# The last stage of a vision tower on one core: where the expert shares are spread, in what order a turn is issued, and when its weights are loaded

## The reference, cut to what matters

```
out = attention among the 8 heads' vectors, softmax(q.k * 16**-0.5) over the heads of one token, times v
y   = x + merge(heads) @ w_proj.T + b_proj           # heads regrouped over tokens
f   = layernorm(y) * ln_scale + ln_bias
routed: a group gate picks one of 2 groups, a softmax over its 4 experts, the top 2 of them, shares renormalised
shared = swiglu(f @ shared_in_w.T) @ shared_out_w.T + shared_out_b
h      = swiglu(f @ expert_in_w.T)                   # 256 values, the same for all 8 experts
y + shared + sum over e of share[e] * (h @ expert_out_weight[e].T + expert_out_bias[e])
```

## Time and profile before

| | |
|---|---|
| median of 3 runs | 2949.59 us |
| the profiled execution | 2955.88 us |
| its span | 2954.1 us |
| stage A, stage B, stage C (from the trace) | 0 to about 1580, to about 1921, to 2954 us |
| PE, DVE, POOL, ACT busy over the span | 83%, 83%, 67%, 51% |
| mean granted TensorE clock | 0.924 of full |

### The profile page before, as it was taken

The page is one execution under the profiler, slowest core; times in us unless marked ns, Lnnn a source line. Parts: engine busy times, 40 slices in busy tenths (PEclk is TensorE's granted clock), DMA queues, the critical chain, the costliest instruction groups (busy, mean ns, idle before and its releaser), DMA issues. The chain is left out here.

```text
span 2954.1 us, 25221 instructions
## 1 busy us (share of the span) xinstructions
PE 2455.6 (83%) x6718; PEld 1146.3 (39%) x6718; DVE 2447.7 (83%) x3527; ACT 1511.1 (51%) x2542; POOL 1978.0 (67%) x1008
## 2 busy tenths in 40 slices
PE   6899898898998898988973068438999999998998
PEld 2344444444444444444431033213444444444443
DVE  4999999999999999999997822137888888888875
ACT  5666666666666666676652134234444433443332
POOL 3888888888888887888882068755555555555540
PEclk9999999999999999999996579758999999999999
DMA  2333323323333323324231024310000000000000
GB/s 83 110 94 98 109 92 105 106 87 117 94 99 107 100 91 108 103 87 119 89 102 51 0 50 71 36 51 22 29 29 29 29 29 29 29 29 29 26 22 11
DMA packets 169758, 199.27 MB, mean 67 GB/s; under 512 B 38969, under 2 KB 156946, under 8 KB 169490
## 3 DMA queue, kind: packets, MB, share of 16 engines
q1 hardware_dynamic: 158354, 189.27, 20.9%
q0 software_dynamic: 11264, 8.40, 2.2%
HBM read 164.37 MB, written 33.25 MB: 67 GB/s over the span
## 5 line engine op out<-in xcount | busy, mean ns | idle before, releaser
L905 POOL TENSOR_TENSOR a_hc<-a_h,a_cs 128x896 f32<-128x896 f32 (+1 forms) x448 | 891.6, 2002 | 182.1 <-DVE a_h L744 181.2
L360 PE MATMUL a_y_bank<-a_hc,a_ident 128*128 128x448 f32 (+1 forms) x1792 | 766.7, 562 | 14.7 <-POOL a_hc L905 13.6
L537 ACT ACTIVATE a_da<-a_dt,a_neg_a 128x448 f32<-128x448 f32 (+1 forms) x896 | 548.4, 632 | 331.3 <-DVE a_h L744 330.3
L744 DVE TENSOR_TENSOR_SCAN a_h<-a_da,a_h,a_dbx 128x448 f32<-128x448 f32 x528 | 583.1, 1134 | 14.2 <-ACT a_da L537 11.9
L360 PEld LDWEIGHTS a_y_bank<-a_hc,a_ident 128*128 128x128 f32 x1792 | 344.1, 196 | 359.9 <-issue 287.2
L2086 POOL TENSOR_TENSOR c_prod<-c_prob,c_qkv 128x1024 f32<-128x1024 f32 x100 | 280.7, 2849 | 274.6 <-DVE c_prob L1973 274.6
L1670 PE MATMUL c_p_ACC<-c_sc,c_w_ex 128*128 128x512 f32 x800 | 365.4, 594 | 0.0
L2079 POOL TENSOR_TENSOR c_prod<-c_qkv 128x1024 f32<-128x1024 f32 x100 | 231.9, 2341 | 152.7 <-ACT c_qkv L1754 152.7
L728 DVE TENSOR_TENSOR a_dbx<-a_dtx,a_b_bank 128x896 f32<-128x896 f32 (+1 forms) x308 | 328.5, 1067 | 4.5 <-PE a_b_bank L353 0.7
L1947 DVE TENSOR_TENSOR c_sc<-c_hid,c_p_CB 128x1024 f32<-128x1024 f32 x200 | 239.9, 1214 | 69.6 <-PE c_p_CB L1662 67.1
L893 POOL TENSOR_TENSOR a_dbp<-a_dtx,a_bs 128x896 f32<-128x896 f32 (+1 forms) x140 | 269.7, 1936 | 0.3
(11 more groups left out here) (297 smaller groups left out, 3688.3 us busy)
## 6 DMA issues: line engine op xcount, KB each, us to landing
a_cs<-c_rows SPq DMA_DIRECT2D x96, 896.0 KB, 5.3
a_bs<-c_rows SPq DMA_DIRECT2D x24, 1120.0 KB, 5.7
a_cs<-c_rows SPq DMA_DIRECT2D x16, 900.0 KB, 4.4
c_x<-h_rows SPq DMA_DIRECT2D x25, 256.0 KB, 2.8
heads<-c_ot SPq DMA_DIRECT2D x25, 256.0 KB, 2.3
c_dealt<-heads SPq DMA_DIRECT2D x200, 32.0 KB, 1.9
rolled<-c_res SPq DMA_DIRECT2D x25, 256.0 KB, 2.1
h_rows<-a_th SPq DMA_DIRECT2D x24, 224.0 KB
```

Of the source, the lines that this page charges most:

```text
L360: pe.matmul(y_bank[:, d, 0:g.w], ident[:], hc[:, (g.i * NS + n) % HC_RING, d, 0:g.w], start=(n == 0), stop=(n == NS - 1)).then_inc(s_sum, 1)
L537: act.activation(da[:, k % DA_RING, 0:g.w], dt[g.slot][:, d, 0:g.w], ACT.Exp, scale=neg_a[:, d * NS + n:d * NS + n + 1]).then_inc(s_da, 1)
L744: dve.tensor_tensor_scan(h[:, n, d, 0:g.w], da[:, (g.i * 2 * NS + k) % DA_RING, 0:g.w], x, state, ALU.mult, ALU.add).then_inc(s_scan, 1)
L905: pool.tensor_tensor(hc[:, (q.i * NS + n) % HC_RING, :, 0:q.w], h[:, n, :, 0:q.w], cs[:, n % C_RING, 0:q.w].unsqueeze(1).to_broadcast([P, ...
```

## The change

Shares: `turn_choice` now leaves the shares as f32 on partitions 96 to 103. ACT copies them to `c_s`; SP writes them to memory (`share_out`, 16 KB) and, once they have landed, reads them back with `partition_broadcast` in two DMAs of four experts each (`share_in`: 4 x 512 f32 on 128 partitions, 1 MB each, 2 MB a turn) into `c_all`, a ring of four. `spread`, `split_mid`, `middle_choice`, `split_low`, the banks CB0 and CB1, `picks` and `sel_e` are gone. The two banks hold `hx`, the 256 expert rows, which `hidden(2)` and `hidden(3)` now write to PSUM; since there is one `hx`, they wait for the last `scale` of the group before. The bias product takes bf16 parts instead of f32.

Residual: in `project` the four products with the identity become PE transposes of `x` and stand ahead of the wait for `dealt`; only the projection itself is behind it.

SP's turn, which was load, store, heads out, heads in, is now: load, `share_out`, `heads_out`, `store_last`, `share_in`, `heads_in`.

Order: the lists of PE, ACT and DVE and `BANK_ORDER` are written anew. DVE's turn begins with `choose_experts`; all four `scale` steps after `less_top` stand around `probs`; `hidden(2)` follows `scale(7)`. PE's experts follow each other after `project` with `center`, `up(7)` and `variance` between the fifth and the seventh; ACT turns `row_scale` ahead of `score_exp`, `column_scale` ahead of `norm_rows`, and `affine` ahead of `silu_table`.

Weights: the tiles of stage C's constants are allocated before stage B's; SP issues their loads in stage B before the weights of its third expert, DVE clears `bias9` in round 6 of stage B's search and builds the derived constants when its part of stage B is over. POOL's four fills at the start of stage B now wait for DVE's `n_high`.

```diff
+            if e == 2:
+                progs["c_load"](sp)                      # stage B's sync
+            if r == 6:
+                progs["c_clear"](dve)                    # stage B's vector
+        pool.wait_ge(s_dve, progs["n_high"])             # ahead of POOL's fills
...
+            def share_out():
+                if X is not None:
+                    sp.wait_ge(s_c_s, X + 1)
+                    sp.dma_start(share_rows[X % 2], c_s[SHARE:SHARE + E1, :]).then_inc(s_rows[X % 2], 16)
+            def share_in():
+                if X is not None:
+                    sp.wait_ge(s_rows[X % 2], (X // 2 + 1) * 16)
+                    for half in range(2):
+                        if X >= 2:
+                            for e in range(half * EG, half * EG + EG):
+                                scaled(sp, X - 2, e)
+                        r = X % 2 * 2 + half
+                        sp.dma_start(c_all[:, r, :, :], share_rows[X % 2][half * EG:(half + 1) * EG, :].partition_broadcast(P)
+                                     ).then_inc(s_all[r], 16)
+            load()
+            share_out()
+            heads_out()
+            store_last()
+            share_in()
+            heads_in()
...
             def project():
+                    for j in range(GT):
+                        pe.matmul(p[:, j * P:(j + 1) * P], x[N % 3][:, j, :], ident[:], is_transpose=True,
+                                  start=(j == 0), stop=False, skip_group_check=True)
                     pe.wait_ge(s_dealt[N % 2], (N // 2 + 1) * (16 * 8))
-                    for j in range(GT):
-                        mm = pe.matmul(p[:, j * P:(j + 1) * P], x[N % 3][:, j, :], ident[:], start=False, ...)
...
             def hidden(i):
+                    if i >= 2 and U:
+                        scaled(dve, U - 1, E1 - 1)
+                    product = hid[U % 2][:, i, :] if i < 2 else hx[:, i - 2, :]
...
             def scale(e):
-                    dve.tensor_tensor(sc[:, k % SC_RING, :, :], hid[X % 2][:, 2:4, :],
-                                      tile_of(f"cb{e}", X)[:].unsqueeze(1).to_broadcast([P, 2, GW]), ALU.mult
+                    dve.tensor_tensor(sc[:, n % SC_RING, :, :], hx[:], shares(dve, X, e), ALU.mult
...
PE:   turn_n3 up0 qkv0 qkv1 up1 up2 turn_choice gates turn_o qkv2 up3 qkv3 up4 shared up5 up6 biases
      project expert0..5 center up7 variance expert6 expert7
ACT:  keep_n3 silu0 qkv0 keep_choice qkv1 keep_o qkv2 silu1 qkv3 silu2 silu3 exp_table gate_exp row_scale
      score_exp keep_h3 square column_scale norm_rows affine silu_table
DVE:  choose_experts values2 values3 hidden0 finish_last stats scores0 choose_group hidden1 scores1 scores2
      scale0 scale1 scale2 scores3 scale3 less_top scale4 scale5 probs scale6 scale7 hidden2 less_mean
      values0 hidden3 rescale values1
```

More of the change, by code:

```diff
@@ L1 @@
 from contextlib import ExitStack
+from dataclasses import dataclass
 import numpy as np
@@ L1406 @@
 NGATE = 2 + E1
-NC = 104
-BANK_ORDER = (("up0", "W0", "U"), ("up1", "W1", "U"), ("n3", "T", "A"), ("up2", "W0", "U"), ("up3", "W1", "U"),
[5 rows of a table removed]
+BANK_ORDER = (("n3", "T", "A"), ("up0", "W0", "U"), ("qkv0", "M", "A"), ("qkv1", "T", "A"), ("up1", "W1", "U"),
[3 rows of a table added]
 STAGES = ("X", "U", "N", "A", "L")
@@ L1435, in bank_table @@
     return nth
-def phase_c(nc, ctx, mem, a, h_rows, out, after_b, progs):
+SHARE, PARTS = 96, (0, 32, 64)
+KB = PARTS[-1] + E1 + 1
+@dataclass
+class Fixed:
+    ident: object
+    cen_w: object
+    mean_w: object
+    w_qkv: object
+    w_proj: object
+    w_up: object
+    w_so: object
+    w_ex: object
+    w_gate: object
+    gate_b: object
+    cols: object
+    eps_cols: object
+    earlier: object
+    later: object
+    bias9: object
+    bias_b: object
+    cc: object
+    s_in: object
+    s_const: object
+    loads: int
@@ L1486, in phase_c @@
     act_half = [sb(f"act_half{i}", [P, GW]) for i in range(2)]
-    hid = [sb(f"hid{s}", [P, 4, GW]) for s in range(2)]
-    cc = sb("cc", [P, GT, P])
-    c_t = sb("c_t", [E1 + 1, GW])
+    hid = [sb(f"hid{s}", [P, 2, GW]) for s in range(2)]
     c_b = sb("c_b", [P, GW], BF16)
+    c_s = sb("c_s", [P, GW])
+    c_all = sb("c_all", [P, ALL_RING, EG, GW])
     sc = sb("sc", [P, SC_RING, 2, GW])
@@ L1494, in phase_c @@
     heads = [nc.dram_tensor(f"heads{s}", [P, 8, GT * 16], F32, kind="Internal").ap() for s in range(2)]
-    banks = {n: ps("p_" + n, [P, 512]) for n in ("T", "R", "M", "W0", "W1", "ACC", "CB0", "CB1")}
+    share_rows = [nc.dram_tensor(f"share_rows{s}", [E1, GW], F32, kind="Internal").ap() for s in range(2)]
+    banks = {n: ps("p_" + n, [P, 512]) for n in ("T", "R", "M", "W0", "W1", "ACC")}
+    hx = ps("hx", [P, 2, 512])
     route = banks["R"]
@@ L1532, in phase_c @@
     s_sq, s_lv, s_r12, s_fl = map(sem, ("sq", "lv", "r12", "fl"))
-    s_route, s_gexp, s_c_b, s_c_r, s_c_m, s_comb, s_ex = map(
-        sem, ("route", "gexp", "c_b", "c_r", "c_m", "comb", "ex"))
-    LOADS = 13
+    s_route, s_gexp, s_c_s, s_comb, s_ex, s_sc = map(
+        sem, ("route", "gexp", "c_s", "comb", "ex", "sc"))
+    s_rows = [sem(f"rows{s}") for s in range(2)]
+    s_all = [sem(f"all{r}") for r in range(ALL_RING)]
     R_DIF, R_END = 8, 24
@@ L1552, in tile_of, with product_done, scaled, shares @@
         return banks[nth[use, c][0]]
+    def product_done(eng, c, e):
+        if e == E1 - 1:
+            result(eng, "acc", c)
+        else:
+            eng.wait_ge(s_ex, c * (E1 - 1) + e + 1)
+    def scaled(eng, c, e):
+        eng.wait_ge(s_sc, c * E1 + e + 1)
+    def shares(eng, c, e):
+        r = c % 2 * 2 + e // EG
+        eng.wait_ge(s_all[r], (c // 2 + 1) * 16)
+        return c_all[:, r, e % EG, :].unsqueeze(1).to_broadcast([P, 2, GW])
     def sync(sp):
-        def store(c):
-            taken(sp, "acc", c)
-            sp.dma_start(out[:, c * GW:(c + 1) * GW], res[c % 2][:]).then_inc(s_res[c % 2], 16)
@@ L1559, in sync @@
         after_b(sp)
[L1560 to L1564, removed]
-        for X, U, N, A, L in turns:
[L1566 to L1578, removed]
-                    sp.dma_start(dealt[s][j * DH:(j + 1) * DH, :, :],
-                                 heads[s][:, j, :].rearrange("(h d) c -> d h c", d=DH)).then_inc(s_dealt[s], 16)
@@ new lines, in sync, with load, store, store_last @@
+        for X, U, N, A, L in turns:
+            def load():
+                if L is not None:
+                    if L >= 3:
+                        result(sp, "proj", L - 3)
+                    sp.dma_start(x[L % 3][:], h_rows[L * GW + SHIFT:(L + 1) * GW + SHIFT, :].rearrange(
+                        "(j p) d -> p j d", p=P)).then_inc(s_x[L % 3], 16)
+            def store(c):
+                if c is not None and c >= 0:
+                    taken(sp, "acc", c)
+                    sp.dma_start(out[:, c * GW:(c + 1) * GW], res[c % 2][:]).then_inc(s_res[c % 2], 16)
+            def store_last():
+                if X:
+                    store(X - 1)
+            def heads_out():
+                if N is not None:
+                    taken(sp, "o", N)
+                    sp.dma_start(heads[N % 2], ot[:]).then_inc(s_heads[N % 2], 16)
+            def heads_in():
+                if N is not None:
+                    s = N % 2
+                    sp.wait_ge(s_heads[s], (N // 2 + 1) * 16)
+                    for j in range(8):
+                        sp.dma_start(dealt[s][j * DH:(j + 1) * DH, :, :],
+                                     heads[s][:, j, :].rearrange("(h d) c -> d h c", d=DH)).then_inc(s_dealt[s], 16)
+            def share_out():
[18 more added lines that the diff above has]
+            heads_in()
```

286 lines of the change are left out of this document (143 added, 143 removed), and 8 rows, old and new, of the table BANK_ORDER.

## The result

| | before | after |
|---|---|---|
| median (runs) | 2949.59 us (7: 2947.46 to 2956.58) | 2966.71 us (7: 2963.41 to 2974.23) |
| profiled execution, its span | 2955.88, 2954.1 us | 2966.71, 2964.9 us |
| mean granted TensorE clock | 0.924 | 0.916 |

The ratio is 1.0061, 95% interval 1.0046 to 1.0076: slower, by 17 us of median and 11 us between the two profiled executions. The forecast was +38.9, 2988.5 us. The sign and the mechanism (the dealing is held up, and the idle costs the clock) held; the size did not.

What follows compares the result with a forecast made beforehand. Neither PE nor DVE is full; a ring of waits sets each turn. 22 x (40.0 - 37.9) = +46.2, +3.4, -10.0, -2.3 and +1.6 give +38.9 on the median 2949.6: 2988.5 us, range 2890 to 3015.

Steps and rivals of the forecast that it cites:

- ramp: First two turns, before the dealing starts: residual gain and later `norm_rows` cancel, 0, between -6 and +6 us.
- first queued turn: The first turn with dealing: it lands late behind the shares, +3.4 us.
- The ring: Steady turn from projection through experts, softmax, value products and heads back to projection: 40.0 us against 37.9.
- the clock's term: PE idles 5 us before each projection, so the lower clock level adds 2.8 us to every turn.
- The queue: In SP's queue the dealing waits behind two share broadcasts: projection at 37.2 us instead of 33.8.
- The share transfer: Two 1 MB broadcasts, scaled by bytes from a 896 KB one, keep the DMA engines busy 6.75 us.
- The tail: After the last projection nothing hides the shares' way: 79.9 us against 78.3, +1.6 (0 to +8).
- Start and stage B: Weights loaded earlier gain 10.0 us at stage C's start; POOL's fills held back gain 2.3 us in stage B.
- Work removed: Busy time a turn falls on PE from 35.1 to about 32 us, on DVE from 31.8 to about 30.6.
- The first (dealing not held up): Rival: small DMAs pass the broadcasts in SP's queue; ring 34.6 us, about 2866 us in all; chance 15%.
- The second: Rival: dealing held up but PE's clock stays, or the idle is short; ring 37.2 us, 2927 us; chance 20%.

Runs made afterwards that it cites:

- e3_fill: The changed kernel with four unused 512-column matmuls on PE ahead of the residual transposes: 2924.4 us, ratio 0.9907.
- e1_half: The changed kernel with one of the two share broadcasts issued behind the dealing: 2866.2 us, ratio 0.9711.
- e10_first: The changed kernel with all eight dealing transfers issued ahead of both broadcasts: 2988.0 us, ratio 1.0115.
- e8_queue: The kernel before with two unused 1 MB broadcasts issued by SP ahead of the dealing every turn with heads out: 3045.4 us, ratio 1.032.
- e12_448: The changed kernel with broadcasts of 448 of 512 columns of each share row, the rest left at zero: 2972.9 us, one run.
- e7: The kernel before with only the residual transposed ahead of the wait for the dealt heads: 2935.7 us, ratio 0.9943.
- e9: The kernel before with the residual transposes ahead of the projection's wait and `up(6)` ahead of the projection: 2908.0 us, ratio 0.9849.
- e5_half_table: The changed kernel with the second broadcast behind the dealing and ACT's silu table load moved behind `keep_n3`: 2856.4 us, ratio 0.967.
- e6: The changed kernel with only the weights' loads put back at the start of stage C: 2985.8 us, ratio 1.011.
- e2_small: The changed kernel with each broadcast repeating one row instead of four, 256 KB each: 2894.7 us, ratio 0.9801.

## Why the prediction had the sign and not the size

| step | predicted | measured, between the two profiled spans |
|---|---|---|
| start, to the first projection | -12.3 | 1963.68 - 1977.37 = -13.7 |
| first two turns (ramp 0, first queued turn +3.4) | +3.4 | 56.49 - 64.68 = -8.2 |
| 22 turns | 22 x (40.0 - 37.9) = +46.2 | 22 x (39.49 - 37.90) = +34.9 |
| last projection to the end | +1.6 | 76.0 - 78.3 = -2.3 |
| sum | +38.9 | +10.8 |

(The first projection before, the third and the last in the sums of before are from its trace at 1977.37, 2042.05 and 2875.80.)

*The ring: the mechanism right, the clock's term too large, and luck in the sum.* In the mean of the 22 turns:

| | forecast | after |
|---|---|---|
| projection to heads out, full clock | 26.05 | 26.67 (e3_fill) |
| what the clock adds to it | 2.8 | 1.87 |
| heads out to projection, queued | 11.15 | 10.95 |
| turn | 40.0 | 39.49 |

The step that failed is the clock's price. I took the 2.8 us from one turn of before with passes of 2.05 us and applied them to all. Measured are 1.9 us, so 22 x 0.9 = 20 us too much. That the row of 22 turns is only 11 us off is in part luck: the way from projection to heads out, without the clock, is 0.6 us longer than my sum, which gives 14 us back. (The forecast's ring of 40.0 is the sum of its three rows; e3_fill lost the clock in two turns, so that 1.87 is a little low.)

*The queue: right.* I had 3.4 us for it (33.8 to 37.2). From heads out to projection are 10.95 us in after, 8.21 with one broadcast ahead (e1_half) and 7.44 with none (e10_first): 2.7 for the second broadcast, 3.5 for both. On the old lists two broadcasts give 2.5 (e8_queue).

*The share transfer: too long, and it mattered little.* I scaled the 896 KB row by bytes to 6.75 us. By rows, of which a 1 MB broadcast has as many (512), it is 2 x 2.95 = 5.90, and e12_448 shows no gain from shorter rows. The engines' busy share gives 6.1 us a turn, within 0.4 (0.24 x 39.49 in after less 0.09 x 37.90 before). Quiet turns show it, 10.2 to 10.5 us from heads out to projection; but in half the turns the issues or landings slip by up to 2.3 us, and the mean is only 0.2 below my 11.15. The Trainium skill, "DMA: Bandwidth & Descriptors", "Bandwidth", has its 341 GB/s for DMAs issued from GpSimd, and these are SP's. The estimate by it, 6.15 us, was nearer than my sum.

*The first two turns were priced at 0 for the lists and gave 10.3.* This step failed as well, and with it 10 of the 28 us between forecast and measurement. e10, the changed lists with nothing queued ahead of the dealing, has 54.40 us there (1964.82 to 2019.22) against 64.68: 10.3 less, and the queue in after gives back 2.1 (56.49), not 3.4. I looked only at the residual and `column_scale`. Before, `keep_h3` stands on ACT behind `exp_table`, that behind `silu(3)`, and that behind `up(6)`, which is behind the projection. The chain of waits through the second of the two turns, before and then after (start, us, what):
```profile
2008.89 2.05 PE c_p_M L1681 x2
2010.94 1.71 PE c_p_M L1685 x8
2012.64 1.18 PE c_p_W L1603 x2
2013.85 0.60 ACT c_act_half L1748
2014.46 1.28 ACT L1784
2015.75 0.70 ACT c_h L1811
```
```profile
1990.14 1.14 PE c_p_T L1793 x2
1991.30 0.69 ACT c_h L1909
```
`keep_h3` starts 6.86 us after the projection in before and 1.16 in after, since the residual and the ups are done by then. In the first of the two turns, where no `up(6)` exists yet, it is 3.79 and 2.11 us, and in the last turn 6.5 and 2.1 (2882.26 behind 2875.80, 2891.04 behind 2888.93). e7 and e9 divide the 10.3: the transposes take 2.1 us off the two turns, `up(6)` another 2.8; 5.4 are left. In the first turn, two up projections at the low clock (3.78 us in e9) stand ahead of the turned `n` in the old lists and behind it in the new; that part was only read, not tried, and what makes the rest stays open. The order of a list that I had read as "written anew" needed the same working as the ring.

*The tail: forecast +1.6, measured -2.3.* The same `up(6)`, again a step of the list that I hadn't priced, takes 3.7 us off it (78.6 in e7, 74.9 in e9). The longer way of the shares is there too: DVE waits 3.22 and 6.57 us for `c_all` in the last two turns, where spreads gave 0 and 0.56 on the first scale, and after ends 1.1 behind e9.

*Start and stage B: right.* The weights gave 12.78 - 3.07 = 9.7 (10.0). The stretched pass is gone: 0.57 us in after against 1.93, and again 0.57 in e1, e3, e5 and e6. The wait of the fills was not taken away by itself, so that it does this is read, not shown.

*Work removed: right for PE, wrong for DVE.* PE is busy 31.55 us in the turns of e1_half at the full clock, where I had about 32. I had DVE's work falling from 31.8 to 30.6 us a turn. It rose to 32.5, and 2.5 of that are the stretched `less_mean` (told under e5_half_table). In the rows shown of after DVE ends nothing of the ring, so there it cost nothing that I can point to.

*Rivals.* The first (dealing not held up), 2866, is the time of e1 by another order of issue (its ring 35.12 and not 34.6, which the first turns make up); I had weighed whether the queue lets small transfers pass, and not that the changed kernel was one exchange away from it. The second, that the clock stays or costs nothing, is refuted by the passes of 2.08 us in after and by e3.

*The median.* The profiled execution of before was 6.3 us above its median and that of after at its median. That is why the median shows 17 and the spans 11; both are far from 38.9.

## What to carry to other kernels

Where a small transfer that ends a wait and a large one share a queue, give each a date, and split the large one around the small: here that is worth 100 us of 2967, and putting either one wholly first loses it. Price each new idle of the tensor engine with the clock that it costs, and where it can't be removed try filling it. When a list of steps is reordered, work out the first and last turns step by step too; they have other waits than the steady ones.

## What the runs showed of the hardware

- A broadcast of one 2 KB row to 128 partitions, 256 KB, lands after 4.8 us in the median, and one of four rows, 1 MB, after 5.0 (e2_small, e1_half). The cost is not in the bytes alone; why a single source row is so slow was not tried.
- Rows of 1792 and of 2048 bytes take the same time (e12_448). While the engines were busy they moved 2.84 MB in 8.05 us in after, 353 GB/s, and 2.58 MB in 8.18 us in e12_448, 316 GB/s; stage A's rows of 1792 bytes had 0.918 MB in 2.95 us, 311 GB/s.
- Idles of PE between about 1.8 and 3.7 us went either way: behind 2.01 us in one turn of e5_half_table and 3.26 in before the passes ran at the lower level, behind 3.35 in after (the third row above) they did not. Behind all of 3.8 us and more they did, in whole or in part. The clock cost after 1.9 us a turn in the mean (projection to heads out, against e3_fill).
- Matmuls of no use shortened a kernel by 42 us.
- `hidden` takes 0.69 us in the mean when it writes to PSUM and 0.68 when it writes to SBUF (after), the price that no row of before had.
- A DVE instruction of 4 columns that began just inside one of POOL's products lasted until the product ended: 2.71 us, against 0.17 in before (told under e5_half_table).
